# Two graph-attention layers on one core: the adjacency and x's rows loaded by three engines' queues instead of two

## The reference

```python
# layer 0 (h = x)
src = h @ a1;  dst = h @ a2
e = src[:, None] + dst[None, :]
e = jnp.where(e > 0, e, 0.01 * e)
attention = softmax(jnp.where(adj > 0, e, NEG_INF), axis=1)
x = layernorm(x + attention @ h)
# layer 1: the same with wh = x @ weight_w in place of h, and a bias
x = layernorm(x + attention1 @ wh + bias)
```

## Time and profile before

| | before |
|---|---|
| median of 3 runs | 512.47 us (512.09 to 514.31) |
| the profiled execution | 512.94 us |
| its span | 511.1 us |
| PE busy | 445.8 us (87%) |
| DVE (VectorE) busy | 401.3 us (78%) |
| ACT (ScalarE) busy | 397.5 us (78%) |
| POOL (GpSimd) busy | 85.8 us (17%) |
| DMA packets | 87.71 MB, mean 172 GB/s |

### The profile page before, as it was taken

One profiled execution on the slowest core, in us unless ns is written; L12 is line 12 of the kernel. 1 busy time (PEld: TensorE's weight loads), 2 busy tenths in 40 slices (PEclk: granted clock), 3 DMA queues, 4 the chain that ended last, 5 costly groups with the idle time before them and its releaser, 6 DMA issues.

```text
span 511.1 us, 11789 instructions
## 1 busy us (share of the span) xinstructions
PE 445.8 (87%) x4420; PEld 416.2 (81%) x4420; DVE 401.3 (78%) x712; ACT 397.5 (78%) x619; POOL 85.8 (17%) x68
## 2 busy tenths in 40 slices
PE   0799678979979798997969989999999999989891
PEld 0479668969978796997869869999999998989791
DVE  3679999889898998989887989775766657574854
ACT  2685279777998888789873749889898989898941
POOL 0002211415133051412403200000101010101010
PEclk9987978988999799898989859999999999999897
DMA  7999999999999999999953001102020111102000
GB/s 198 245 224 277 275 263 293 338 299 333 312 307 315 328 321 306 322 321 299 320 173 125 1 1 44 42 9 86 12 82 19 73 34 58 57 35 75 20 12 10
DMA packets 80294, 87.71 MB, mean 172 GB/s; under 512 B 7298, under 2 KB 76162, under 8 KB 80258
## 3 DMA queue, kind: packets, MB, share of 16 engines
q1 hardware_dynamic: 45602, 52.98, 36.3%
q10 hardware_dynamic: 34656, 34.21, 24.7%
HBM read 77.74 MB, written 9.44 MB: 171 GB/s over the span
## 4 chain that ended last, share of the span: by engine, by line
issue 50%; DVE 21%; DMA 21%; PE 3%; POOL 2%; SPq 1%; ACT 0%; POOLq 0%; ACTq 0%; DVEq 0%
DMA stage<-in_adj 19%; DVE narrow L791 5%; DVE turned L803 3%; PE acc L418 2%; DVE pos L817 2%; POOL small L968 2%; DMA xn<-in_x 2%; DVE num L861 1%; DVE num L854 1%; DVE red L847 1%; DVE kept L728 1%; DVE bn L866 1%; DVE kept L725 1%; DVE neg L820 1%; SPq L225 1%
## 5 line engine op out<-in xcount | busy, mean ns | idle before, releaser
L557 ACT ACTIVATE neg<-srow,dcol 128x512 int8 (+1 forms) x512 | 352.8, 878 | 11.7 <-issue 8.2
L418 PE MATMUL acc<-xy_old,pos 128*128 128x195 bf16 x1024 | 195.2, 260 | 26.3 <-POOL pos L979 22.1
L418 PE MATMUL acc<-xy_old,neg 128*128 128x195 bf16 x1024 | 195.0, 261 | 0.0
L418 PE MATMUL acc<-stage,pos 128*128 128x195 bf16 x1024 | 179.4, 249 | 4.8 <-DVE red L829 4.8
L418 PE MATMUL acc<-stage,neg 128*128 128x195 bf16 x1024 | 179.4, 249 | 0.0
L418 PEld LDWEIGHTS acc<-xy_old,pos 128*128 128x128 fp8e4 x1024 | 106.2, 104 | 34.8 <-issue 33.5
L418 PEld LDWEIGHTS acc<-stage,pos 128*128 128x128 fp8e4 x1024 | 101.2, 99 | 9.9 <-issue 9.7
L418 PEld LDWEIGHTS acc<-xy_old,neg 128*128 128x128 fp8e4 x1024 | 105.7, 103 | 1.4
L418 PEld LDWEIGHTS acc<-stage,neg 128*128 128x128 fp8e4 x1024 | 100.7, 98 | 0.2
L791 DVE TENSOR_SCALAR narrow<-stage 128x4096 uint8<-128x4096 int32 x32 | 74.0, 2314 | 17.7 <-DMA stage<-in_adj 16.9
L820 DVE TENSOR_TENSOR neg<-neg,kept 128x1024 uint32<-128x1024 uint32 x32 | 39.2, 1224 | 44.7 <-ACT neg L557 44.1
(11 more groups left out here) (117 smaller groups left out, 326.6 us busy)
## 6 DMA issues: line engine op xcount, KB each, us to landing
stage<-in_adj ACTq DMA_DIRECT2D x64, 512.0 KB, 9.1
stage<-in_adj SPq DMA_DIRECT2D x64, 512.0 KB, 9.4
spill<-turned SPq DMA_DIRECT2D x16, 512.0 KB, 8.1
turned<-spill SPq DMA_DIRECT2D x16, 512.0 KB, 3.9
out<-x1s SPq DMA_DIRECT2D x8, 128.0 KB, 1.9
xn<-in_x SPq DMA_DIRECT2D x1, 768.0 KB, 16.7
kept<-in_x SPq DMA_DIRECT2D x4, 128.0 KB, 3.8
kept<-in_x ACTq DMA_DIRECT2D x4, 128.0 KB, 4.6
```

Of the source, the lines that this page charges most:

```text
L418: last = nc.tensor.matmul(acc[:, r, c * XW:(c + 1) * XW], masks[c][:, t // BYTES, t % BYTES, r * P:(r + 1) * P], xy[layer][:, g * GT + t, ...
L557: last = nc.scalar.activation(o[:, t // BYTES, t % BYTES, :], srow[:, bass.ds((s % 2) * 512, 512)], ACT.Sign, bias=dcol[:, layer, col:col ...
```

## The change

Each granule's four ranges of partitions are dealt out anew. SP issues range 0 alone, and keeps the writes to `spill`. ACT issues range 1 and the lower half of range 3. GpSimd issues range 2 and the upper half of range 3, with semaphores of its own (`pool_loaded`), for which VectorE's narrow now waits too. Both loads of x's rows go from SP to GpSimd, one ahead of and one behind GpSimd's shares of the first two granules. In GpSimd's list each issue (`load_next`) stands ahead of a `positive`, and at the border of two stretches it stands between `inverse_std` and `positive(s, 3)`.

```diff
+        SP_ROWS = ((0, 0, Q),)
+        ACT_ROWS = ((1, 0, Q), (3, 0, Q // 2))
+        POOL_ROWS = ((2, 0, Q), (3, Q // 2, Q))
+        LOADS = len(SP_ROWS + ACT_ROWS)
...
-        def load(queue, quarters, s, g):
+        def load(queue, parts, s, g, done=loaded):
             rows = rows_of(adj, s, GR, Q)
-            for a in quarters:
+            for a, q0, q1 in parts:
                 c = g * (NA * JC) + a * JC
-                queue.dma_start(stage[Q * a:Q * a + Q, g % SLOTS, :].rearrange("p (m j) -> p m j", j=JC),
-                                rows[:, :, c:c + JC]).then_inc(loaded[g % SLOTS], 16)
-
...
+                queue.dma_start(stage[Q * a + q0:Q * a + q1, g % SLOTS, :].rearrange("p (m j) -> p m j", j=JC),
+                                rows[q0:q1, :, c:c + JC]).then_inc(done[g % SLOTS], 16)
...
-            load_rows(sp, slice(0, RB))
-            load(sp, LOWER, 0, 0)
-            load_rows(sp, slice(RB, IB // 2))
-            load(sp, LOWER, 0, 1)
+            load(sp, SP_ROWS, 0, 0)
+            load(sp, SP_ROWS, 0, 1)
...
-                    load(sp, LOWER, s, g)
+                    load(sp, SP_ROWS, s, g)
...
-                load(act, UPPER, s + (g + SLOTS) // NG, (g + SLOTS) % NG)
+                load(act, ACT_ROWS, s + (g + SLOTS) // NG, (g + SLOTS) % NG)
...
-                dve.wait_ge(loaded[g % SLOTS], 16 * NA * (s * (NG // SLOTS) + g // SLOTS + 1))
+                dve.wait_ge(loaded[g % SLOTS], 16 * LOADS * (s * (NG // SLOTS) + g // SLOTS + 1))
+                dve.wait_ge(pool_loaded[g % SLOTS], 16 * len(POOL_ROWS) * (s * (NG // SLOTS) + g // SLOTS + 1))
...
+            load_rows(pool, slice(0, RB))
+            for g in range(SLOTS):
+                load(pool, POOL_ROWS, 0, g, pool_loaded)
+            load_rows(pool, slice(RB, IB // 2))
+
+            def load_next(s, g):
+                pool.wait_ge(narrowed, s * NG + g + 1)
+                pool.sem_inc(pool_turn, 1)
+                load(pool, POOL_ROWS, s + (g + SLOTS) // NG, (g + SLOTS) % NG, pool_loaded)
...
+            def body0(s, last=False):
+                load_next(s + 1, 0)
+                positive(s, NG - 1)
+                for g in range(1, NG):
+                    if g < SLOTS or not last:
+                        load_next(s + 1, g)
+                    positive(s + 1, g - 1)
                 inverse_std(0, s)
-                positive(s + 1, 3)
+
+            with pool.Fori(0, NS - 2) as s:
+                body0(s)
```

More of the change, by code:

```diff
@@ L153, in gat_kernel @@
         loaded = [sem(f"loaded{g}") for g in range(SLOTS)]
+        pool_loaded = [sem(f"pool_loaded{g}") for g in range(SLOTS)]
         s_x = [sem(f"s_x{n}") for n in range(2)]
@@ L219, in row_at @@
             return bass.ds(s // 2 * (2 * RB) + s % 2 + 2 * r, 1)
-        def load(queue, quarters, s, g):
+        SP_ROWS = ((0, 0, Q),)
+        ACT_ROWS = ((1, 0, Q), (3, 0, Q // 2))
+        POOL_ROWS = ((2, 0, Q), (3, Q // 2, Q))
+        LOADS = len(SP_ROWS + ACT_ROWS)
+        LOWER, UPPER = (0, 1), (2, 3)
+        def load(queue, parts, s, g, done=loaded):
             rows = rows_of(adj, s, GR, Q)
-            for a in quarters:
+            for a, q0, q1 in parts:
                 c = g * (NA * JC) + a * JC
-                queue.dma_start(stage[Q * a:Q * a + Q, g % SLOTS, :].rearrange("p (m j) -> p m j", j=JC),
-                                rows[:, :, c:c + JC]).then_inc(loaded[g % SLOTS], 16)
-        LOWER, UPPER = (0, 1), (2, 3)
+                queue.dma_start(stage[Q * a + q0:Q * a + q1, g % SLOTS, :].rearrange("p (m j) -> p m j", j=JC),
+                                rows[q0:q1, :, c:c + JC]).then_inc(done[g % SLOTS], 16)
         def load_tiles(queue, quarters):
@@ L266, in _ @@
                 sp.wait_ge(narrowed, g - SLOTS + 1)
-                load(sp, LOWER, 0, g)
+                load(sp, SP_ROWS, 0, g)
             with sp.Fori(1, NS) as s:
@@ L507, in _ @@
             act.dma_start(idf[:, :], ident).then_inc(s_a, 16)
-            load(act, UPPER, 0, 0)
+            load(act, ACT_ROWS, 0, 0)
             def load_next(s, g):
                 act.wait_ge(narrowed, s * NG + g + 1)
-                load(act, UPPER, s + (g + SLOTS) // NG, (g + SLOTS) % NG)
+                load(act, ACT_ROWS, s + (g + SLOTS) // NG, (g + SLOTS) % NG)
             def tables0():
@@ L521, in tables0 @@
                 signs(0, 0, 0)
-                load(act, UPPER, 0, 1)
+                load(act, ACT_ROWS, 0, 1)
                 for t in range(2, NS):
@@ L982, in _ @@
             for g in range(NG - 1):
+                load_next(0, g)
                 positive(0, g)
[L984 to L987, removed]
+            load_next(0, NG - 1)
+            def body0(s, last=False):
[5 more added lines that the diff above has]
+                    positive(s + 1, g - 1)
                 inverse_std(0, s)
-                positive(s + 1, 3)
+            with pool.Fori(0, NS - 2) as s:
+                body0(s)
+            body0(NS - 2, last=True)
+            positive(NS - 1, NG - 1)
             inverse_std(0, NS - 1)
```

## The result

The changed kernel takes 611.35 us (median of 4 runs, 606.21 to 619.41), the kernel before 513.18 us in the same session: a ratio of 1.188 (95% interval 1.179 to 1.197). It is 98 us slower. One run of it, 619.41 us, fell in a slower state of the chip, as did one of experiment 4's and two of experiment 5's: the medians given are of all runs, the ratios and the table's differences for these kernels leave such runs out (here 96 us are then left of the 98). The prediction had 518.5 us in a range of 500 to 530.

What follows compares the result with a forecast made beforehand. VectorE and its waits for adj bound layer 0, TensorE layer 1. Six borders +8.5, the start -2.35 and the first stretch -0.4 made +5.8 on 512.94 us, stated as 518.5 us, range 500 to 530.

Steps and rivals of the forecast that it cites:

- What bounds the kernel: Layer 1 by TensorE, untouched; layer 0's stretches, 30.09 us on average, by VectorE and its 2.37 us of waits for adj.
- The balance: Layer 0's stretches: evening out the queues keeps DMA at 346 GB/s and saves VectorE's adj waits, 2.37 us a stretch.
- the DMA gets no faster: Rival: three queues do no more than two, the stretch's two adj waits stay, start's 2.35 us not gained; 521 us, chance 0.10.
- The start: First granules: SP and GpSimd issue adj early, saving VectorE's 2.35 us wait; x's rows on another queue cost nothing, ±1.5 us.
- GpSimd's issues: Stretch borders: two issues, 2.0 us, delay positive(s, 3) and the third narrow; stretch 31.5 us, six borders +8.5 us.
- the prediction's bound from above: GpSimd's two issues at a border: 768 pieces, one by one at 2.5 ns, written twice, 3.8 us.
- it is faster: Rival: both issues under 1.0 us, positive(s, 3) still goes ahead of the second narrow; 499.5 us, chance 0.28.
- nothing to see: Rival: issues take 1.0 to 1.4 us, or go on beside narrow and only pos waits; 511.5 us, chance 0.17.
- The mechanism: Stretch borders: a GpSimd issue caught under VectorE's narrow stands still and goes on behind its end, t0 + 7.6.
- it is much slower: Rival: issues take 3.8 us, stretch 33.3 us, or GpSimd holds up narrow; 529.5 us, chance 0.15.
- if the second narrow still waits as long, the balance was not worth what I took: Test on the profile after: the second narrow's 0.83 us wait for adj in a stretch should be nearly gone.

Runs made afterwards that it cites:

- experiment 4: Kernel before, SP with ranges 0 and 1, ACT 2 and 3, but ranges 1 and 3 each as two DMAs of 16 partitions: 565.56 us, 1.097.
- experiment 5: Changed kernel without GpSimd DMAs: SP loads ranges 0 and 2 and x's rows, ACT range 1 and both halves of range 3: 626.48 us.
- Experiment 1: Kernel before with only the pairing changed: SP loads ranges 0 and 2, ACT 1 and 3, both in the same half: 582.05 us, 1.1325.
- 2: As Experiment 1, but ranges 1 and 2 change places in SBUF, so the queues write opposite halves: 514.19 us, 1.0003.
- experiment 6: As experiment 5, but ACT's list is turned, range 3's halves before range 1, so SP and ACT write opposite halves: 553.04 us, 1.075.
- experiment 3: Changed kernel with whole ranges: SP range 0, ACT range 2, GpSimd ranges 1 and 3: 548.91 us, 1.069.
- Experiment 7: As experiment 3, but SP has range 0, ACT range 1 and GpSimd both upper ranges, 2 and 3: 555.23 us, 1.079.
- experiment 8: Kernel before with the 16 writes to spill issued by GpSimd, each behind a positive, adj loaded as before: 514.33 us, 1.001.
- Experiment 9: Kernel before plus two almost empty GpSimd DMAs at each place where the changed kernel issues its loads: 515.39 us, 1.0006.
- 10: Changed kernel with both loads of x's rows back on SP's queue: 617.1 us, 1.200.
- 11: Kernel before with SP's second load of x's rows moved behind its shares of granule 1 of adj: 519.78 us, 1.012.

## Why the prediction was wrong

**What bounds the kernel.** That held: layer 1 did not change, and layer 0 is paced by VectorE and by what it waits for. The view that misled is the earlier trace rows.

**The balance: the step that failed.** "So the most that the new deal can give is nearly all of the 2.37 us a stretch." It read one queue at 191 GB/s and two at 346 as an effect of their number. In the kernel before, the number of queues and the number of halves written go together, so those rows can't tell them apart; and the change breaks the second: it adds a queue and puts two of them in one half. The rate, which the forecast let rise from 316 to 346 GB/s, fell to 231 and 227. The waits did not go from 14.2 us to nearly none: over the kernel they went from 16.9 to 94.5. Its parts, tried one by one (difference of the medians of one session, for 5 of the two runs named there; the number of the experiment in brackets):

| what is changed in the kernel before | against it |
|---|---|
| both queues in one half at a time (1) | +68.6 us |
| the same, each in its own half (2) | +0.7 |
| half of adj's bytes in 16-partition DMAs (4) | +51.0 |
| the changed kernel's ranges, on SP and ACT (5) | +107 |
| the same, opposite halves (6) | +38.2 |
| GpSimd with whole ranges (3; 7) | +35.5; +40.4 |
| spills on GpSimd (8) | +0.8 |
| GpSimd's issues, without the data (9) | +0.6 |

They don't add up to 98 and needn't: they are costs of the same resource. But 5 has more than the whole loss with GpSimd's DMA left out, and 8 and 9 have nothing of it with only GpSimd's DMA put in. The cause is where the ranges lie and who writes them together. That the halves and the narrow pieces slow a load is shown by 1 and 2, 4, 5 and 6; how the 98 us of the changed kernel divide between them, the turn by packet and the late start of GpSimd's data is argued from its windows. The expectations had the directions and not the sizes: 1 came out 8 us below its range, 3, 6 and 10 came out 3 to 5 us above, 4 some 15 and 5 some 21 above.

The rival "the DMA gets no faster", and the rule of the Trainium skill (page DMA: Bandwidth & Descriptors, section "Rules for kernel authors") on spreading DMAs over queues that stood beside it, came nearest in mechanism: a third queue brought no rate, and experiment 8 says so directly (317 GB/s from 100 to 220 us, as before). But it kept the waits of before as they were. No case of the prediction let the rate fall, and so no case came near 611 us; the highest, 529.5, was high for another reason, the issues.

**The start.** Forecast -2.35 us, measured +11.3 to the first narrow. The sign is wrong; x's rows were the wrong suspect (experiments 10 and 11), and that GpSimd's large packets stand beside x's tiles is what is left. It was not tried by itself.

**GpSimd's issues, "the term that decides".** It decided nothing. The size was off: 2.0 us for the two, measured 1.27 at the border, and by line, first in the changed kernel and then in experiment 3, where all are of 512 KB:

```profile
L232 POOL DMA_DIRECT2D stage<-in_adj x64: 563/611/702, 2.3 to 341.9; - x64
```

```profile
L232 POOL DMA_DIRECT2D stage<-in_adj x64: 650/651/2397, 2.4 to 284.5; - x64
```

The first row mixes two sizes: the 512 KB issues take 0.65 us or a little more, the 256 KB ones 0.56. So twice the pieces cost 0.09 us, and the prediction's bound from above, which counted pieces, was far off. Its rival "it is faster" put the point at which it decides at 1.0 us for the two, "nothing to see" at 1.0 to 1.4. Experiment 9, with 1.05 us, is 1.0006: that rival's "nothing to see" was right about the issues taken alone.

The mechanism was right, only rarely met. The one long issue of experiment 3 began 0.14 us into a narrow and ended 0.25 us behind it:

```profile
168.09 2.29 DVE L795 TENSOR_SCALAR narrow<-stage 128x4096 uint8<-128x4096 int32 x1 [1.26 <-DMA stage<-in_adj]
168.23 2.40 POOL L232 DMA_DIRECT2D stage<-in_adj  x1 [5.22 <-issue]
```

Experiment 7 has one such, 1.97 us, and experiment 8 two of 16, 2.32 and 2.33. Where GpSimd loads adj, an issue waits for `narrowed` and so comes right behind a narrow; in the changed kernel only one of the 64 overlaps the next narrow, and it had begun first. The Trainium skill's page SBUF — State Buffer, section "SBUF: two separate sides", gives about 620 ns for such a DMA alone and about 3100 ns under VectorE's lock; it doesn't say whether it means the issue. The 0.56 to 0.65 us are near the first figure; the 2.40 us are less than the second, and their end just behind the narrow's agrees with its mechanism.

The other way round, a narrow that begins while GpSimd works is lengthened: 2.77 us in experiment 9, 3.62 where an issue and then a `pos` stood before it, 3.54 in the changed kernel. Experiment 1, with no DMA on GpSimd, has one of 2.81 beside a `pos`, so this doesn't take an issue. It had no cost that could be measured in experiment 9, so it was not the rival "it is much slower" either.

**What would have shown it.** The prediction's own test, "if the second narrow still waits as long, the balance was not worth what I took", is what happened, and more: 0.83 us became 4.63.

Left open: how the rate comes about when q0 and one hardware queue write opposite halves (250 GB/s in experiment 3, 314 GB/s or more with two hardware queues); and whether a third queue of small packets, with its ranges kept to the idle half, would win the 14 us of waits that remain. No run loaded adj through GpSimd's queue in smaller packets, so this wasn't tried. No kernel of these beats the kernel before.

## What to carry to other kernels

Before dealing a load anew, write down for each queue which half of the partitions (0 to 63, 64 to 127) it writes at each moment: two queues in opposite halves moved 339 GB/s, two in the same half 211, and where pieces of 16 partitions were in flight it was down to 143 GB/s even with the queues in opposite halves. Two rates in one trace that go with "one queue" and "two queues" may go with something else that the old kernel never varied; if the change varies it, price that case too. And by the counts here a queue with larger packets takes its share of an engine by packet, not by byte, so don't give it the half that the others must wait for, nor put it beside a load that the start hangs on.

## What the runs showed of the hardware

- The rate by destination, with 1 KB rows: one half 191 to 211 GB/s whether one queue or two write it, both halves 339 to 346. While a piece of 16 partitions was in flight it was 115 (one us of the changed kernel) and 143 (three us of experiment 6).
- GpSimd's queue moves the same 1 KB rows in packets of 3.3 to 4 KB on average, SP's and ACT's in about 1 KB. With all three at work they had 90, 91 and 92 packets in 2 us; beside ACT's, in experiment 7, GpSimd's had as many packets and 3.8 times the bytes.
- A DMA issue on GpSimd is 0.65 us for 512 KB, 0.56 for 256 KB and 0.50 for 1 KB and less (medians), and 1.97 to 2.40 us when it begins under a narrow of VectorE (experiments 3, 7 and 8). The 64 of experiment 9 cost nothing that can be measured.
- A narrow of 2.29 us took up to 3.62 us when it began while GpSimd was at work.
- The order of the DMAs in one engine's list, nothing else, was worth 68 us (experiments 5 and 6).
